# How many row gathers may be in flight: from eight to two, in the stair passes and the MLP edge pass of a four-layer graph network

## The reference

```
x = LN(x + L0)   L0: sum over edges, by src, of x[dst] * d[src] * d[dst]      (d = 1/sqrt(degree))
x = LN(x + L1)   L1: sum over edges, by dst, of (x @ W[relation])[src]         (8 relations)
x = LN(x + L2)   L2: an MLP on each edge's (x[src], x[dst], weight), summed by src; an MLP on each node
x = LN(x + L3)   L3: relu(conv(x, W1)), then conv( . , W2), each a normalised sum by dst, plus x @ We
```

## Time and profile before

| | us |
|---|---|
| median of 3 timed runs | 5206.31 |
| lowest and highest of them | 5196.57, 5220.39 |
| span of the profiled execution, first to last instruction | 6179.1 |
| POOL busy in it | 3107.2 (50%) |
| PE busy in it | 3566.1 (58%) |
| DVE busy in it | 2253.1 (36%) |
| ACT busy in it | 1380.4 (22%) |

### The profile page before, as it was taken

One profiled execution on the slowest core, in us unless ns is written; L12 is line 12 of the kernel. 1 busy time (PEld: TensorE's weight loads), 2 busy tenths in 40 slices (PEclk: granted clock), 3 DMA queues, 4 the chain that ended last, 5 costly groups with the idle time before them and its releaser, 6 DMA issues. The chain is left out here.

```text
span 6179.1 us, 72632 instructions
## 1 busy us (share of the span) xinstructions
PE 3566.1 (58%) x19811; PEld 2738.2 (44%) x19811; DVE 2253.1 (36%) x4940; ACT 1380.4 (22%) x3101; POOL 3107.2 (50%) x2834
## 2 busy tenths in 40 slices
PE   3333362466756663455547667977993345717448
PEld 2111121465722322454336554676772344716447
DVE  7444592233555651221701101243452122503128
ACT  0000000000133440111401014633440122303125
POOL 2555506676166776777365533000115777377733
PEclk8555575555576776776555558999996676858769
DMA  3000041111145663111524345565563111211114
GB/s 104 2 2 2 10 149 35 37 46 39 56 188 208 232 245 131 20 22 22 195 66 114 101 115 158 175 201 175 196 231 135 21 22 22 101 24 19 23 26 149
DMA packets 311485, 589.50 MB, mean 95 GB/s; under 512 B 178785, under 2 KB 180702, under 8 KB 292960
## 3 DMA queue, kind: packets, MB, share of 16 engines
q1 hardware_dynamic: 146819, 465.93, 21.3%
q0 software_dynamic: 87808, 66.01, 5.9%
q10 hardware_dynamic: 76506, 53.12, 2.6%
HBM read 286.68 MB, written 310.95 MB: 97 GB/s over the span
## 5 line engine op out<-in xcount | busy, mean ns | idle before, releaser
L1303 PE MATMUL e_ring<-e_msgs,e_hot 128*128 x6272 | 1162.3, 347 | 1182.0 <-issue 1124.2
L1303 PEld LDWEIGHTS e_ring<-e_msgs,e_hot 128*128 128x128 f32 x6272 | 1077.1, 248 | 1270.4 <-issue 1264.6
L1028 POOL DMA_INDIRECT e_msgs<-y,index_D x784 | 880.2, 1123 | 402.7 <-issue 226.9
L1147 DVE TENSOR_TENSOR e_hot<-iota,keys_D 128x2048 f32<-128x2048 f32 x147 | 337.1, 2293 | 1472.9 <-remote 732.5
L603 POOL DMA_INDIRECT list_D<-d_place,d_target x392 | 456.5, 1165 | 318.7 <-DVEq L557 202.0
L1028 POOL DMA_INDIRECT e_msgs<-y,index_S x392 | 400.5, 1022 | 377.9 <-DVE index_S L1133 194.6
L603 POOL DMA_INDIRECT list_S<-s_place,s_target x392 | 390.8, 997 | 363.4 <-DVEq L557 248.0
L1627 POOL DMA_INDIRECT m_far<-x,index_S x392 | 390.0, 995 | 353.0 <-DMA pairs_by_edge<-m_far 225.4
L1028 POOL DMA_INDIRECT e_msgs<-x_by_relation,index_D x392 | 446.5, 1139 | 170.2 <-issue 110.9
L1777 PE MATMUL m_ring<-rows,m_hot 128*128 x1568 | 374.3, 423 | 213.4 <-issue 211.2
L2453 POOL TENSOR_TENSOR n_sq<-n_cent 128x1792 f32<-128x1792 f32 x14 | 44.4, 3175 | 826.4 <-DVE n_cent L2348 826.4
(11 more groups left out here) (386 smaller groups left out, 5706.0 us busy)
## 6 DMA issues: line engine op xcount, KB each, us to landing
x_by_relation<-d_stage SPq DMA_DIRECT2D x98, 1024.0 KB
m_keyrow<-keys_by_step SPq DMA_DIRECT2D x49, 512.0 KB
rows<-pairs_by_edge SPq DMA_DIRECT2D x49, 512.0 KB
messages<-rows SPq DMA_DIRECT2D x98, 256.0 KB
rows<-messages SPq DMA_DIRECT2D x49, 512.0 KB, 4.0
sums<-m_stage ACTq DMA_DIRECT2D x98, 256.0 KB, 3.8
n_in<-sums SPq DMA_DIRECT2D x14, 1792.0 KB
s_xc<-x_padded SPq DMA_DIRECT2D x28, 448.0 KB, 3.8
```

The lines of the kernel that those rows point to most:

```text
L1028: pool.indirect_dma_start(out=msgs[:, (i % HELD) * D:(i % HELD + 1) * D], out_offset=None, in_=source, in_offset=bass.IndirectOffsetOnAxis ...
L1147: nc.vector.tensor_tensor(hot[g % 2][:, :, :], bc(nodes[:, 0:P].unsqueeze(1), [P, GS, P]), bc(order["keys"][:, g * GS:(g + 1) * GS].unsque ...
L1303: mm = nc.tensor.matmul(ring[:, bass.ds(bucket, step)], hot[g % 2][:, k, :], moved, start=False, stop=False, skip_group_check=True)
```

## The change

A gather waits for the landing of gather `i - 2`: all but the last gather before it have landed when it is issued. The constant is new, and the two waits change; all else stays, the eight semaphores too.

```diff
+FLYING = 2
...
-                if i >= SLOTS:
-                    pool.wait_ge(s_land[i % SLOTS], before + 16 * (i // SLOTS))
+                if i >= FLYING:
+                    pool.wait_ge(s_land[(i - FLYING) % SLOTS], before + 16 * ((i - FLYING) // SLOTS + 1))
                 pool.indirect_dma_start(
                     out=msgs[:, (i % HELD) * D:(i % HELD + 1) * D], out_offset=None, in_=source,
...
-                if i >= SLOTS:
-                    pool.wait_ge(s_land[i % SLOTS], before + 16 * (i // SLOTS))
+                if i >= FLYING:
+                    pool.wait_ge(s_land[(i - FLYING) % SLOTS], before + 16 * ((i - FLYING) // SLOTS + 1))
                 pool.indirect_dma_start(
                     out=far[:, (i % AHEAD) * D:(i % AHEAD + 1) * D], out_offset=None, in_=source,
```

## The result

The kernel with the change takes 5841.74 us (median of 4 runs, 5834.28 to 5877.43), against 5204.95 us (4 runs) for the kernel before on the same chip: a ratio of 1.1229, 95% interval 1.1188 to 1.1271. It is slower, as forecast, by 637 us where 254 us were forecast; 5842 us lies beyond the range, which ended at 5620 us.

A forecast was written before the change was run, and what follows sets the result against it. POOL's issuing of gathers was taken to bound the passes. Slower cadence 180 us, load stretches 34 us and MLP bursts 40 us sum to 254 us: 5206 + 254 = 5460 us, range 5230 to 5620 us.

The forecast's parts named there:

- The ring as a cover: Rival: POOL's waits for a full ring take in part of the added time, about +85 us, 5290 us; chance 0.13.
- the growth of the profiled span to 6250 us: Profiled execution grows from 6179 us by only some 70 us, as waits for ring and spill take in additions.
- Load stretches: Start of the second and fourth passes, node rows loading: cadence becomes 3.24 us, 34 us lost together.
- the 29 us of the sum: Time at the second pass's start taken at the 3.24 us cadence: 18 us lost, the same in the fourth.
- The cadence in the stairs: Stair passes: a start every 1.36 us instead of 1.25; 34 us in each pass by destination, 39 in the first.
- (392 - 86) x 0.11: Each pass by destination: 392 gathers, less 86 that go free around long gathers, lose 0.11 us each: 34 us.
- The MLP edge pass: The pass's loss: 39 us from the slower cadence plus 40 us while bursts of keys and stores fill the DMA engines.
- I take 40 us: MLP edge pass: loss chosen for bursts of key loads and stores, between bounds of 0 and 119 us.
- upper bound of 119 us: MLP edge pass: all 195 us of full DMA engines go at the 3.24 us cadence, losing 0.61 us each.
- Gathers of 2.6 us stay as many.: Sign for the profile after: the number of long gathers does not change; no added time was forecast for them.

The follow-up runs named there:

- second profile of before: The kernel before, unchanged, run and profiled once more: 5210.20 us, ratio 0.9998, profiled span 5205.5 us.
- e1: Not a run: the second gathering pass, a stair pass by destination that loads node rows; POOL idle 195 us with the change, 120 to 121 before.
- e3: Not a run: the fourth gathering pass, a stair pass by destination that loads node rows; POOL idle 192 us with the change, 120 to 121 before.
- e4: Not a run: the last gathering pass, a stair pass by destination without node-row loads; POOL idle 181 us with the change, 120 to 121 before.
- e0: Not a run: the first gathering pass, a stair pass whose build reads a table from PSUM; POOL idle 192 us with the change, 120 to 121 before.
- fly3: The changed kernel with the constant at 3, so gather i waits for the landing of gather i-3: 5343.09 us, ratio 1.0247 to the kernel before.
- swap_again: The changed kernel with the landing's wait put ahead of the room or spill wait: 5860.63 us, against 5917.59 us for the changed kernel on that chip.

## Why the prediction missed: right in kind, wrong in size

**The direction and the mechanism of the wait held.** POOL sets the end of each gathering pass, a gather follows the landing of the one before the last, and each us of POOL's cadence is one of the kernel: 644 us in the stretches, 637 in the time. Seen landing and start were sized well (forecast 2.45 + 0.27; measured 2.41 + 0.24). By the Trainium skill, "DMA: Bandwidth & Descriptors", section "Anatomy of one DMA — SWDGE (gpsimd) path", as estimated ahead of the result, a landing would have come after 2.08 us and the wait would have cost nothing; the traces don't agree (2.41 us, and pairs of 2.65 us and more), and the forecast was right to go by the row. The ring as a cover, and the growth of the profiled span to 6250 us that hung on it, fell with the second profile of before.

**Load stretches.** Forecast: starts about 3.2 us apart while the node rows load. POOL at the start of e1, after:

```profile
1859.92 0.97 POOL L1029 DMA_INDIRECT e_msgs<-x_by_relation,index_D  x1 [0.30 <-issue]
1865.31 0.95 POOL L1029 DMA_INDIRECT e_msgs<-x_by_relation,index_D  x1 [4.42 <-DMA e_msgs<-x_by_relation,index_D]
1866.57 2.84 POOL L1029 DMA_INDIRECT e_msgs<-x_by_relation,index_D  x1 [0.30 <-DMA e_msgs<-x_by_relation,index_D]
1871.14 0.95 POOL L1029 DMA_INDIRECT e_msgs<-x_by_relation,index_D  x1 [1.73 <-DMA e_msgs<-x_by_relation,index_D]
1875.11 0.95 POOL L1029 DMA_INDIRECT e_msgs<-x_by_relation,index_D  x1 [3.02 <-DMA e_msgs<-x_by_relation,index_D]
1877.74 0.95 POOL L1029 DMA_INDIRECT e_msgs<-x_by_relation,index_D  x1 [1.69 <-DMA e_msgs<-x_by_relation,index_D]
```

From 1859.92 to 1877.74 us are five steps of 3.6 us on the mean; gathers 3 to 11 start 3.1 us apart in e1 and 3.2 in e3. But the full stretch is over after some 13 gathers, so the first 20 are 2.35 and 2.50 us apart, and e1 and e3 have 14 and 11 us more idle time than e4, 25 us together, where 34 were forecast. The mechanism, the pace and roughly the size were right; that the first 20 gathers go at that pace was not (the 29 us of the sum hold nine at 3.24 us).

**The cadence in the stairs: 141 us forecast (34 in each pass by destination, 39 in e0), some 254 measured** (279 less those 25). The step that failed is "(392 - 86) x 0.11". Two things were missing. From the 129th on, every eighth gather pays 0.48 us more for its second wait (idle time beyond the gap at these gathers is 19 to 21 us a pass; undoing it gave 57 us over all five passes). And the landing of a quiet moment was put in the sum, where late ones count more: in e0 SP sees landings at a median of 2.42 and a mean of 2.57 us, and with two in flight a late one is lost time, while an early one is held back by the 1.25 us that POOL needs anyway. With the mean, the sum for e0 is 392 x ((2.57 + 0.24) / 2 - 1.25) = 61 us, and with 33 x 0.48 = 16 us more 77, where 72 were measured and 39 forecast. This second part is argued from the landings; no run separates it.

**The MLP edge pass: 79 us forecast (39 of cadence, 40 of bursts), 216 measured.** The step is "I take 40 us", and its upper bound of 119 us was too low as well. Both were read off an execution in which the pass lasted 734 us at a DMA share of 0.38 to 0.47. Undisturbed, it packs the same traffic into 524 us at 0.60, where a gather's semaphore is full 3.7 us after its start, on the mean (median 3.5). Eight in flight hid that. In after, slowed to 737 us, it is still 3.2 us: (3.2 + 0.24) / 2 - 1.25 = 0.47 us for each gather, which by this estimate makes 184 of the 216 us, and the second wait at 41 gathers 20 more.

**"Gathers of 2.6 us stay as many."** They did, 49 in each pass by destination, but they went from 2.0 to 3.05 us: 144 us forecast at nothing, 149 with the busy time of the other two passes. The prediction took their length for a property of the gather. It is set by where VectorE's build falls. Both are now released by the same landing, POOL directly and VectorE by SP's count of it, so each build meets a gather at its very start. The trace of after shows that one landing sets the phase: in 125 of 144 builds the build starts 0.18 us after SP saw a landing, and the gather that the same landing frees starts 0.24 us after it. In fly3, where the waits are rare, the phase and the length are those of before. That the build makes the gathers long is shown by the runs without builds and in pieces.

Sum of the misses: 113 in the stairs' cadence, less 9 in the load stretches, 137 in the MLP edge pass, 149 in POOL's busy time: 390 us, which with the forecast's 254 makes the 644 of the stretches.

## What to carry to other kernels

Where one queue issues a chain of transfers and its cadence sets the end, keep in flight what covers the late landings under the heaviest traffic beside it, not the median of a quiet stretch: here eight cost nothing, three 2.5% and two 12%, and four to seven were not measured. The mean alone isn't enough: three leave a landing 3 x 1.25 - 0.24 = 3.51 us, and the MLP edge pass's mean landing in fly3 is 3.63 us, which would lose (3.63 - 3.51) / 3 x 392 = 16 us; it loses 114 us. Before reading prices from a profile, hold its span against the timed runs, and take another where they differ. And look at what lengthens the issues themselves: four short builds instead of one long one took 2.9% off the kernel before, without touching the transfers.

## What the runs showed of the hardware

- A GpSimd gather that starts while VectorE compares two SBUF tables stands until that instruction ends, plus 0.82 us; one that started first is not touched (0.95 us), and the build takes its 2.29 us all the same. Where the build has one table in PSUM (e0), the gathers that start during it take 0.95 us. The Trainium skill, "SBUF — State Buffer", section "Who interferes with whom", says that a VectorE instruction with two SBUF inputs contends with a GpSimd instruction that reads SBUF, that one with a single SBUF input, outside VectorE's 2-port modes, does not, and that the order of issue decides which one blocks: for the gather these traces agree, 147 of 147 and 79 of 79 in before's second profile; that a build is held by a gather under way shows in no build's length. The same section of the Trainium skill infers that such a compare leaves the writing of descriptors alone; here a gather's issue is held by it all the same.
- A gather with one wait starts 0.24 us after another engine saw the landing it waits for, one with two waits 0.72 us after it when the landing's wait stands last, and 0.24 us when it stands first (swap_again).
- The same change costs 637 us in one set of runs and 703 us in another, where landings are seen 0.06 us later, while the kernel before takes 5205 and 5215 us in the two. With eight in flight such a difference hardly shows. Of the traces that nothing disturbed, only that of after has the earlier landings, so whether the chip makes them isn't settled.
